# Row halves of TensorE for two products, and sums moved from VectorE to GpSimd, in a causal-filter and attention kernel

## The reference

```python
# layer 0 (32 decay rates D)
ctx = causal_ema(x, tau_ctx)
wg = sigmoid(concat([x, ctx]) @ Wg.T + bg);  gated = x * wg
h1 = gelu(x @ Wn1.T + bn1)
mod = 0.5 + sigmoid(h1 @ Wn2.T + bn2)                       # one factor per decay rate
traces = causal_ema(gated * mod[..., None], tau_d)          # for each of the 32 rates
temporal = einsum('dbtc,dc->btc', traces, softmax(blend))
gate = sigmoid(temporal @ Wtemp.T + btemp);  soma = gelu(x @ Wsoma.T + bsoma)
out = (soma * gate) @ Wout.T
x1 = x + (out - mean) / sqrt(var + 1e-5) * gamma + beta
# layer 1: q, k, v of x1; per position 32 listed neighbours (a key listed n times counts n times)
#   or all keys with a bias, softmax, values, Wo, and x1 is added
```

## Time and profile before

| | us |
|---|---|
| median of 3 runs (341.52 to 347.49) | 341.86 |
| the profiled execution, its own time | 341.25 |
| its span, first to last instruction | 339.3 |
| start to step 1 (front and step 0) | 47.47 |
| steps 1 to 6 | 119.51 |
| attention | 172.32 |

### The profile page before, as it was taken

The page is one execution under the profiler, slowest core; times in us unless marked ns, Lnnn a source line. Parts: engine busy times, 40 slices in busy tenths (PEclk is TensorE's granted clock), DMA queues, the critical chain, the costliest instruction groups (busy, mean ns, idle before and its releaser), DMA issues. The chain is left out here.

```text
span 339.3 us, 10025 instructions
## 1 busy us (share of the span) xinstructions
PE 317.3 (93%) x3333; PEld 211.4 (62%) x3333; DVE 291.6 (86%) x1500; ACT 215.0 (63%) x458; POOL 224.3 (66%) x279
## 2 busy tenths in 40 slices
PE   7998888999999999999988799999999999999995
PEld 2545254573756557474535576777787877787873
DVE  3895699999898999988788866999999999999982
ACT  6760225566455656555716787788888878888863
POOL 3254164535355453625537768799999999999990
PEclk9996799999999999999999999999999999999999
DMA  6600002015060421301551244565555354301011
GB/s 190 198 3 0 31 0 65 32 49 93 2 139 2 90 52 53 88 0 53 69 74 28 39 93 79 84 120 139 127 100 122 92 123 101 84 5 34 2 34 33
DMA packets 29155, 23.08 MB, mean 68 GB/s; under 512 B 2736, under 2 KB 27824, under 8 KB 29104
## 3 DMA queue, kind: packets, MB, share of 16 engines
q1 hardware_dynamic: 29104, 22.44, 30.3%
HBM read 7.75 MB, written 2.10 MB: 29 GB/s over the span
## 5 line engine op out<-in xcount | busy, mean ns | idle before, releaser
L1566 POOL TENSOR_TENSOR arena<-arena,neg_max 128x512 f32<-128x512 f32 x128 | 129.6, 1042 | 14.3 <-DVE neg_max L1437 13.8
L1437 DVE CUSTOM_DVE_ANT_0 arena<-ps,arena 128x128 f32<-128x128 f32 x512 | 113.6, 286 | 11.6 <-issue 5.8
L1076 ACT ACTIVATE arena<-ps 128x512 f32<-128x512 f32 x128 | 69.6, 597 | 9.0 <-PE ps L775 8.9
L1514 POOL TENSOR_TENSOR arena<-arena 128x448 f32<-128x448 f32 (+6 forms) x56 | 41.1, 735 | 48.5 <-DVE arena L1268 45.1
L775 PE MATMUL ps<-ident_sb,arena 128*128 128x128 f32 x512 | 68.2, 276 | 0.0
L775 PEld LDWEIGHTS ps<-ident_sb,arena 128*128 128x128 f32 x512 | 56.5, 141 | 7.0 <-issue 4.3
L1501 POOL TENSOR_TENSOR arena<-decay_a,arena 128x192 f32<-128x192 f32 x32 | 20.0, 655 | 36.2 <-ACT arena L920 36.2
L1437 DVE DVE_READ_ACCUMULATOR2_ANT neg_max<- 128x1 f32 x512 | 42.4, 83 | 0.0
L791 PE MATMUL ps<-arena 128*32 128x128 f32 x1024 | 41.2, 279 | 0.0
L791 PEld LDWEIGHTS ps<-arena 128*32 128x32 f32 x1024 | 24.0, 109 | 6.9 <-issue 0.3
L761 PE MATMUL ps<-arena 48*128 48x128 bf16 x512 | 25.4, 219 | 3.0 <-DVE neg_max L1437 3.0
(11 more groups left out here) (164 smaller groups left out, 584.2 us busy)
## 6 DMA issues: line engine op xcount, KB each, us to landing
...
```

Source lines behind the costliest of these rows:

```text
L1076: act.activation(probT[q % PT_RING], ps[1][:, q % 2, :], ACT.Exp, scale=-1.0)\
L1437: dve.tensor_tensor_reduce(out=neg_t[q % NT_RING][:, cs], in0=ps[0][:, score_bank(c) + slot, cs], in1=nbias[n % 2], scale=1.0, scalar=3.0e ...
L1514: pool.tensor_tensor(a, a, pr_, ALU.add).then_inc(s["lag_added"], 1)
L1566: pool.tensor_tensor(t4, t4, neg_max[:, n % 2, 4 * z:4 * z + 4].unsqueeze(2).broadcast_to([P, 4, P]), ALU.subtract).then_inc(s["shifted"], 1)
```

## The change

- **Modulation** (L481): each of the four matmuls takes only the 64 rows that hold its weights (`half`), sequences 0 and 1 in the lower rows and into bank 0, 2 and 3 in the upper rows and into bank 1, issued in turn 0, 2, 1, 3. ScalarE's tanh reads both banks. The soma product, which uses bank 0, waits for the tanh and stands behind the gate product.
- **Lag pairs**: `f_lag_pair` does lags n and n+1 together: the two 128-row matmuls, then the remainder of lag n on rows 64 to 127 and of lag n+1 on rows 0 to 63. For that ScalarE copies the upper half of `mod_pb` to its lower half (`f_mod_low`), and `lag_b` is filled in rows 0 to 63. Group 0 keeps its own form (`first_lags`). Pairs 0, 2, 4, 6 stand in the step's list; pair 6 behind the output product.
- **Residual**: two operations of 512 elements on GpSimd, at the start of its step, in place of four of 128 on VectorE. In the attention part it stays on VectorE.
- **Counts**: VectorE compares four columns of indices at once (128x512 bf16), two such in each of steps 1 to 4; GpSimd adds them up (`counted`). 1/std on GpSimd moves before lag 7.

```diff
-FIRST_COUNT = (0, 6, 12, 17, 22, 27, K_SPARSE, K_SPARSE)
+FIRST_QUAD = (0, 0, 2, 4, 6, 8, 8, 8)
...
         key_no = sb("key_no", [P, P], BF16)
-        so_far = [sb(f"so_far{k}", [P, P], BF16) for k in range(2)]
+        so_far = sb("so_far", [P, 4, P], BF16)
+        idx_b = sb("idx_b", [P, K_SPARSE], BF16)
...
+        hot = [a.rearrange("p (j k) -> p j k", j=4) for a in (
+            arena[:, at[0] - 4 * P:at[0] - 2 * P].bitcast(BF16), arena[:, at[0] - 2 * P:at[0]].bitcast(BF16))]
...
-                if not at_start(i, m, 2):
-
-                    pe.wait_ge(s["cross_ready"], grp(i, m, 1, -1))
+                if not at_start(i, m, 1):
+
+                    pe.wait_ge(s["modT_tanh"], grp(i, m, 1, 1))
...
-                for b in range(GB):
-                    mm = pe.matmul(bank(u, 1)[:, b * P:b * P + P], wn2_row[:, b, :], h1T[u], start=True, stop=True)
+                    pe.wait_ge(s["cross_ready"], grp(i, m, 1, -1))
+                if at_start(i, m, 1):
+                    pe.wait_ge(s["soma_ready"], 1)
+                two_banks = ps[u][:, 0:2, :]
+                for b in (0, 2, 1, 3):
+
+                    half, c0 = slice(64 * (b // 2), 64 * (b // 2) + 64), (b % 2) * P
+                    mm = pe.matmul(two_banks[:, b // 2, c0:c0 + P], wn2_row[half, b, :], h1T[u][half, :],
+                                   start=True, stop=True)
...
+            def f_lag_pair(i, m, lag):
+
+                u = m % 2
+                if lag == 0:
+                    pe.wait_ge(s["soma_ready"], grp(i, m, 1, 1))
+                    pe.wait_ge(s["mod_part3"], grp(i, m, 1, 1))
+                    pe.wait_ge(s["mod_part1b"], grp(i, m, 1, 1))
+                    if at_start(i, m, 2):
+                        pe.wait_ge(s["vec_step"], vec("w_b2"))
+                        pe.wait_ge(s["act_step"], scal("w_b1"))
+                else:
+                    pe.wait_ge(s["prod_ready"], grp(i, m, Q, lag - 1))
+                pe.matmul(bank(u, 0), lag_a[:, lag, :], mod_pa[u][:], start=True, stop=False)
+                if lag == 0:
+                    pe.wait_ge(s["modn_ready"], grp(i, m, 1, 1))
+                else:
+                    pe.wait_ge(s["prod_ready"], grp(i, m, Q, lag))
+                pe.matmul(bank(u, 1), lag_a[:, lag + 1, :], mod_pa[u][:], start=True, stop=False)
+                if lag == 0:
+                    pe.wait_ge(s["mod_low_ready"], grp(i, m, 1, 1))
+                pe.matmul(bank(u, 0), lag_b[64:128, lag, :], mod_pb[u][64:128, :], start=False, stop=True)\
+                    .then_inc(s["lag_ps"], 1)
+                pe.matmul(bank(u, 1), lag_b[0:64, lag + 1, :], mod_pb[u][0:64, :], start=False, stop=True)\
+                    .then_inc(s["lag_ps"], 1)
...
+                    f_gate_x(i, m + 1)
                     f_soma(i, m + 1)
-                    f_gate_x(i, m + 1)
...
-                f_lags(i, m + 1, range(0, 2))
+                f_lag_pair(i, m + 1, 0)
...
-                f_lags(i, m + 1, range(2, 3))
                 b_crossT(i, m)
-                f_lags(i, m + 1, range(3, 4))
+                f_lag_pair(i, m + 1, 2)
...
-                f_lags(i, m + 1, range(4, 7))
+                f_lag_pair(i, m + 1, 4)
                 if closes:
                     c_less(i, m - 1, 0, 1)
                 b_out(i, m)
+                f_lag_pair(i, m + 1, 6)
                 if closes:
                     c_v(i, m - 1)
-                f_lags(i, m + 1, range(7, Q))
...
-                act.activation(thd[u], bank(u, 1), ACT.Tanh, bias=hb[:, 2:3], scale=0.5).then_inc(s["modT_tanh"], 1)
+                act.activation(thd[u].rearrange("p (k n) -> p k n", k=2), ps[u][:, 0:2, 0:2 * P], ACT.Tanh, bias=hb[:, 2:3], scale=0.5).then_inc(s["modT_tanh"], 1)
...
+
+            def f_mod_low(i, m):
+
+                u = m % 2
+                act.wait_ge(s["mod_part1b"], grp(i, m, 1, 1))
+                act.wait_ge(s["mod_part3"], grp(i, m, 1, 1))
+                act.activation(mod_pb[u][0:64, :], mod_pb[u][64:128, :], ACT.Copy).then_inc(s["mod_low_ready"], 1)
...
                 for r0 in (32, 96):
                     act.activation(lag_a[r0:r0 + 32], w_rest[r0:r0 + 32], ACT.Copy).then_inc(s["act_step"], 1)
+                act.wait_ge(s["vec_step"], vec("w_b2"))
+                act.activation(lag_b[32:64], w_lag[32:64], ACT.Copy).then_inc(s["act_step"], 1)
...
                     f_mod_part1(i, m + 1)
+                    f_mod_part1b(i, m + 1)
                     f_soma(i, m + 1)
                     f_context(i, m + 1)
-                    f_mod_part1b(i, m + 1)
                     f_modulation_n(i, m + 1)
+                    f_mod_low(i, m + 1)
                     f_gate(i, m + 1)
...
-                pro("w_mid", dve.tensor_copy(w_mid[64:96], w_rest[64:96]))
-                pro("w_b2", dve.tensor_tensor(lag_b[64:96], w_rest[64:96], w_mid[64:96], ALU.subtract), waited=False)
+                pro("w_mid", dve.tensor_copy(w_mid[0:96], w_rest[0:96]))
+                pro("w_b2", dve.tensor_tensor(lag_b[0:96], w_rest[0:96], w_mid[0:96], ALU.subtract), waited=False)
...
-                pro("idx_masked", dve.tensor_scalar(idx_m[:], idx_m[:], -1.0, None, ALU.add), waited=False)
+                pro("idx_masked", dve.tensor_scalar(idx_b[:], idx_m[:], -1.0, None, ALU.add))
...
-            def counts(first, last):
-
-                for j in range(first, last):
-                    n = so_far[j % 2][:]
-                    if j < 2:
-                        pro(f"hot{j}", dve.tensor_scalar(n, key_no[:], idx_m[:, j:j + 1], None, ALU.is_equal),
-                            waited=False)
-                    else:
-                        dve.wait_ge(s["vec_step"], vec(f"hot{j - 2}"))
-                        pro(f"hot{j}", dve.scalar_tensor_tensor(n, key_no[:], idx_m[:, j:j + 1], n,
-                                                                ALU.is_equal, ALU.add), waited=False)
+            def counts(r):
+
+                if r > 2:
+                    dve.wait_ge(s["counted"], r - 2)
+                pro(f"hot{r}", dve.tensor_tensor(so_far[:] if r == 0 else hot[r % 2],
+                                                 key_no[:].unsqueeze(1).broadcast_to([P, 4, P]),
+                                                 idx_b[:, 4 * r:4 * r + 4].unsqueeze(2).broadcast_to([P, 4, P]),
+                                                 ALU.is_equal), waited=False)
 
             def late_tables():
-                dve.wait_ge(s["vec_step"], vec(f"hot{K_SPARSE - 1}"))
-                pro("count", dve.tensor_tensor(lncnt[:], so_far[0][:], so_far[1][:], ALU.add))
+                dve.wait_ge(s["counted"], K_SPARSE // 4 - 1)
+                pro("two_counts", dve.tensor_tensor(so_far[:, 0:2, :], so_far[:, 0:2, :], so_far[:, 2:4, :], ALU.add))
+                pro("count", dve.tensor_tensor(lncnt[:], so_far[:, 0, :], so_far[:, 1, :], ALU.add))
...
-                first, last = FIRST_COUNT[2 * i + m], FIRST_COUNT[2 * i + m + 1]
+                first, last = FIRST_QUAD[2 * i + m], FIRST_QUAD[2 * i + m + 1]
                 if closes:
                     b_carries(i, m)
-                    c_residual(i, m - 1)
                     f_mod_parts(i, m + 1)
...
                 if first < last:
-                    counts(first, first + 2)
+                    counts(first)
                 b_temporal(i, m)
                 f_lags(i, m + 1, range(2, 4))
                 if first < last:
-                    counts(first + 2, first + 4)
+                    counts(first + 1)
                 b_mixed(i, m)
-                f_lags(i, m + 1, range(4, 6))
-                if first < last:
-                    counts(first + 4, last)
-                f_lags(i, m + 1, range(6, 7))
+                f_lags(i, m + 1, range(4, 7))
...
+            def c_residual(i, m):
+
+                u = m % 2
+                pool.wait_ge(s["centred"], grp(i, m, GB, GB))
+                pool.wait_ge(s["rstd_ready"], grp(i, m, 1, 1))
+                pool.tensor_tensor(by_row(x1g[u]), by_row(ln[u]), rstd[:, u, :].unsqueeze(2).broadcast_to([P, GB, P]),
+                                   ALU.mult).then_inc(s["scaled"], 1)
+                pool.wait_ge(s["scaled"], grp(i, m, 1, 1))
+                pool.wait_ge(s[f"xb_loaded{u}"], i * 16 + 16 * (m // 2 + 1))
+                pool.tensor_tensor(x1g[u], x1g[u], xb[u], ALU.add).then_inc(s["x1_ready"], 1)
...
+                first, last = FIRST_QUAD[2 * i + m], FIRST_QUAD[2 * i + m + 1]
+                if not at_start(i, m, 1):
+                    c_residual(i, m - 1)
                 f_decayed(i, m + 1, range(GB))
                 if not at_start(i, m, 1):
                     c_keep(i, m - 1)
-                f_lags(i, m + 1, range(1, Q))
+                f_lags(i, m + 1, range(1, 2))
+                if first < last:
+                    counted(first)
+                f_lags(i, m + 1, range(2, 4))
+                if first < last:
+                    counted(first + 1)
```

(9 more changed lines are left out.)

55 lines of the change are left out of this document (21 added, 34 removed).

## The result

The changed kernel is slower: a median of 346.06 us (22 executions, 342.1 to 351.67) against 341.48 (22, 340.57 to 348.5); ratio 1.0093, 95% interval 1.0069 to 1.0117. That is clear of 1, but smaller than the 2% that this kernel's measurement tells from no change. Forecast was 335.5, range 331.8 to 339.6. The profiled execution is one of the eight (351.15 us, span 349.3), so it is read by stages, each beside its granted clock.

A forecast was written before the change was run, and what follows sets the result against it. TensorE's stream plus one loop through VectorE bounds most steps; VectorE holds steps 0 and 1. Gains of 1.8, 1.05, 0.77, 1.6 (steps 3 to 5) and 0.8 sum to -6.0 us: 341.25 to 335.2, stated as 335.5, range 331.8 to 339.6.

The forecast's parts named there:

- Front (costed at nothing): Ahead of the steps: one more ScalarE copy, lying where TensorE waits for VectorE, taken to cost nothing.
- Step 0, -1.8: Step 0, without counts: TensorE's 0.90 us wait for temporal and most of its 1.01 for lag 6 go, -1.8 us.
- The sum for a step like 3: Steps 3 to 5, each: modulation -0.25, lag pairs -0.06, wait -0.58, new wait +0.25, transposes +0.10; -0.54 us.
- wait before lag 6: TensorE's 0.58 us wait for VectorE's lag 4 product; claimed to go, as the output product now stands ahead.
- q's new wait: TensorE at the q remainder, behind the gate product: waits for ScalarE's copy until 123.50, 0.25 us a step.
- f_mod_low at nothing: ScalarE's new copy in each step: covered by TensorE's other work, so no cost; uncovered up to 0.7 us a step.
- Steps 1 and 2, -1.05 and -0.77: Step 1, held by VectorE, falls to 19.7 us (-1.05); step 2 from 19.80 to 19.03 (-0.77).
- Step 6, -0.8: Step 6 falls from 20.22 to 19.4 us; VectorE still makes the tables of counts ahead of it.
- the rival with 2.1: GpSimd's sums of counts take 2.1 us, twice as long, making lag 4 and lag 6 late: 339.2 us, chance 0.12.
- A full drain at each change of form (0.16): TensorE's row-half changes cost the array's full way, 0.16 us, ten a step: 339.4 us, chance 0.13.
- Halves one behind the other: TensorE's row halves do not run at once, since both add into PSUM: 344.4 us, slower; chance 0.05.
- The wait only moves: q remainder and mixed hold the output product as lag 4 did; only steps 0 to 2 gain: 338.0 us, chance 0.08.

The follow-up runs named there:

- experiment 1: The changed kernel run once more, unaltered: 346.09 us, ratio 1.0063 to the kernel before.
- experiment 7: The kernel before with only the front's modulation (groups 0 and 1) in row halves: 350.97 us.
- experiment 8: The kernel before with the front's modulation in row halves, each half issued twice so TensorE stays occupied: 341.34 us, ratio 1.0014.
- experiment 3: The changed kernel with the front's modulation (groups 0 and 1) over 128 rows again, the steps keeping the halves: 342.8 us, ratio 1.0046 to the kernel before.
- experiment 4: VectorE's and GpSimd's part of the change alone (residual, counts), TensorE and ScalarE as in the kernel before: 341.41 us, ratio 0.9995.
- experiment 2: The changed kernel with TensorE's wait for ScalarE's copy of v moved from the carries to the locals: 343.45 us, ratio 1.0019 to the kernel before.
- experiment 12: The changed kernel with v's wait ahead of the locals, 128-row front modulation, tables in mid step 5, 128-row remainders, no f_mod_low: 335.53 us, 0.9852 to the kernel before.
- experiment 6: The changed kernel with only the tables of counts moved to the middle of step 5: 342.34 us, ratio 0.9969 to the kernel before.

## Why the prediction was wrong

It was 10.6 us under the median (335.5 for 346.06), and the sign was wrong too. Most terms of its sum were of the right size; what failed is the list of waits that the new order makes, and three things costed at nothing that were not: the front's modulations, `f_mod_low`, and the tables of counts beside GpSimd's residual.

- **Front (costed at nothing).** In the profiled execution this is the largest miss, in the one near the median (experiment 1) the second. The prediction named the front for one ScalarE copy, and its two modulations not at all. In the profiled execution front and step 0 lose 6.0 us where -1.8 was forecast, in experiment 1 they lose 1.0; experiments 7 and 8 show that the halves bring a wait, and that the clock stays up when it is filled. It was readable in part: the windows of before would have shown 2.4 GHz kept to 26 us, with TensorE occupied without a gap from 8 to 24. That a wait of 0.35 us there would cost the level was not.
- **Step 0, -1.8: near the measured size, but partly by luck.** Experiment 3 begins step 1 by 1.78 earlier, of which step 0 itself gives 1.49. The reason given, no counts in step 0, is worth 0.4 by itself (experiment 4) and leaves the wait of 1.01 as it was. The rest comes only with TensorE's new order as well, which takes that wait away and puts one of 0.74 ahead of the output product.
- **The sum for a step like 3.** Its terms were near: pair 0.64 (0.63), wait before lag 6 gone, q's new wait 0.17 to 0.24 (0.25). Modulation gives 0.17 and not 0.25: 0.90 became 0.64, and the carries ahead of it take 1.02 for 0.93 (107.99 to 108.92 before). What failed is the list of waits: moving v behind the last pair made ScalarE's copy of v the last thing before the carries, +0.41, which ate the gain of 0.40 (experiment 2). Asking "what is late next" only behind the output product was the error; it has to be asked for each step that changes its neighbour.
- **f_mod_low at nothing, "uncovered it costs up to 0.7".** The cover held in steady steps but for 0.17 and not in step 1, where VectorE is late: 0.90 of waiting. In step 1 it costs more than its length of 0.63, since the tanh and x1's copy queue behind its wait. Experiment 12 takes it away: step 1 falls from 21.02 to 20.08, steady steps from 19.16 to 18.99. The halves it serves earn 0.01 a pair (0.64 for 0.65, experiment 12), so the edit is a loss.
- **Steps 1 and 2, -1.05 and -0.77.** Step 2 measured -0.22, and with v's wait moved -0.65. Step 1 measured +0.26; -0.55 with the sums alone, -0.69 in experiment 12. The waits there are 0.64 for VectorE's carries and 0.90 for the copy of x1 turned, where 19.7 left room for some 0.7 in all; how much of it VectorE brings from step 0 was not tested.
- **Step 6, -0.8.** Measured +2.67. "VectorE makes the tables of counts and still does" left out that GpSimd's residual now runs beside them. The contention had been priced for the parts of the modulation (0.6 us) and not for the tables, where it takes 1.7 and, behind TensorE's wait, 1.3 of lower clock (experiment 2). In the execution near the median this is the largest miss. Experiment 6 gives 3.3 us of the step back.
- **VectorE's and GpSimd's sizes were right:** a compare takes 0.68 and 1.21 (0.7 to 1.8 forecast; 2.4 a pair, 1.9 measured), a sum of counts 1.15 (1.1, which leaves nothing of the rival with 2.1), VectorE is freed by 2.08 us. But experiment 4 shows that this freeing was worth 0.4 us in step 0, 0.55 in step 1, 0.23 in step 2 and nothing in a steady step.
- **Attention unchanged, 172.32.** It took 173.5 here, with a clock of 0.91 between 196 and 216 us (experiments 1 and 6, with 173.6 and 173.4, have the same low stretch), and 172.3 to 174.9 over the experiments, with the code untouched. What decides it stays open: experiment 7 has 174.85 without a low clock in that stretch, experiment 6 shows that step 6's delay does not.
- **Rivals.** A full drain at each change of form (0.16) is refuted by 0.64 a pair, which means 0.10. The Trainium skill ("TensorEngine Tiling (Array Packing)", Key Properties) states that a change of tiling mode drains TensorE; what a change costs here is that 0.10. Halves one behind the other: refuted, they start at the same 126.57. "The wait only moves" was nearest: the waits moved, not to the output product but to the carries.

With the four obstacles gone (experiment 12: front, v's wait, tables, copy) the kernel gains 5.8 us, from 341.31 to 335.53. That this is about the forecast sum of -6.0 is in part luck: it is another kernel, without halved remainders and with the tables moved, and its step 6 gives 1.2 where -0.8 was forecast, its front and step 0 1.55 for -1.8, step 1 0.7 for -1.05.
